# Banded-prior attention and two local layers on one core: how a head's result reaches the output projection

## What is computed

```
Q, K, V = (layernorm(x) @ W.T + b), each split into 16 heads of 16
scores  = Q K^T / 4 + lambda * gaussian_mask      (2048 x 2048 for each of 4 x 16 heads)
out     = softmax(scores) V                       (heads side by side again: 2048 x 256)
x1      = x + out @ Wo.T + bo
```

## Time and profile before

| | us |
|---|---|
| median of 3 runs | 5806.74 (5804.14 to 5806.75) |
| the profiled execution | 5799.5, span 5797.7 |
| TensorE busy in the span | 5625.3 |
| VectorE busy | 4845.0 |
| ScalarE busy | 3783.4 |
| GpSimd busy | 2148.8 |
| granted TensorE clock, mean | 0.992 |
| attention loop with its tail | to about 3188 |

### The profile page before, as it was taken

How to read it: one execution, slowest core, us unless ns; L and a number is a source line. 1 busy time by engine, 2 the same in 40 slices (tenths; PEclk the granted TensorE clock), 3 DMA queues, 4 the chain that set the end, 5 groups by cost and what they waited for, 6 DMA issues and landing times. The chain is left out here.

```text
span 5797.7 us, 159698 instructions
## 1 busy us (share of the span) xinstructions
PE 5625.3 (97%) x66524; PEld 3530.3 (61%) x66524; DVE 4845.0 (84%) x10062; ACT 3783.4 (65%) x6455; POOL 2148.8 (37%) x1750
## 2 busy tenths in 40 slices
PE   8999999999999999999999899999999999999999
PEld 3444444444444444444444788888787788888787
DVE  8888898888988888989996888888676888888676
ACT  4766776667766667767776677777333677777333
POOL 3111002111021110020001789988111789988222
PEclk9999999999999999999999999999999999999999
DMA  3111111111011101011010444555100454555111
GB/s 102 28 33 37 30 24 46 33 41 36 19 48 33 37 28 35 19 55 32 19 24 17 112 113 113 114 116 114 41 11 7 110 114 112 114 116 118 52 55 48
DMA packets 257796, 341.53 MB, mean 59 GB/s; under 512 B 41312, under 2 KB 160432, under 8 KB 257072
## 3 DMA queue, kind: packets, MB, share of 16 engines
q1 hardware_dynamic: 257072, 331.32, 23.6%
HBM read 103.90 MB, written 41.94 MB: 25 GB/s over the span
## 5 line engine op out<-in xcount | busy, mean ns | idle before, releaser
L640 ACT ACTIVATE a_pr<-a_w 128x1024 f32<-128x1024 f32 x2048 | 1989.0, 1022 | 772.3 <-PE a_w L508 672.6
L767 DVE TENSOR_REDUCE a_mx<-a_b 128x1 f32<-128x512 f32 x2658 | 1718.3, 685 | 212.9 <-PE a_b L489 210.8
L489 PE MATMUL a_b<-a_kp,a_qp 96*32 96x512 bf16 x16200 | 1460.8, 380 | 58.1 <-DVE a_mx L767 28.3
L508 PE MATMUL a_w<-a_qp,a_kp 99*32 99x512 bf16 x16384 | 1259.2, 379 | 3.5 <-ACT a_pr L640 3.0
L765 DVE CUSTOM_DVE_ANT_0 a_junk<-a_b,a_gw 128x512 bf16<-128x512 f32 x1392 | 954.4, 686 | 160.1 <-PE a_b L489 119.8
L538 PE MATMUL a_po<-a_pr,a_v 128*17 128x512 f32 x8192 | 1070.7, 592 | 0.4 <-ACT a_pr L640 0.4
L489 PEld LDWEIGHTS a_b<-a_kp,a_qp 96*32 96x32 bf16 x16200 | 482.1, 96 | 900.4 <-issue 356.6
L1591 POOL TENSOR_TENSOR l_p<-l_p,l_rc 128x512 f32<-128x512 f32 (+1 forms) x512 | 721.8, 1437 | 27.9 <-DVE l_rc L1489 27.7
L508 PEld LDWEIGHTS a_w<-a_qp,a_kp 99*32 99x32 bf16 x16384 | 464.8, 97 | 400.4 <-ACT a_pr L640 34.4
L898 POOL CAST a_pk<-a_nm 128x16 bf16<-128x16 f32 x64 | 12.6, 197 | 1774.3 <-DVE a_nm L773 1774.3
L1236 PE MATMUL l_G<-l_wqkv,l_hT 128*128 128x512 f32 x2304 | 618.6, 414 | 29.5 <-DVE l_hT L1432 23.1
(11 more groups left out here) (227 smaller groups left out, 8887.8 us busy)
## 6 DMA issues: line engine op xcount, KB each, us to landing
l_qs<-l_qT SPq DMA_DIRECT2D x512, 128.0 KB, 2.3
l_kh<-l_kT SPq DMA_DIRECT2D x512, 128.0 KB, 2.4
l_kl<-l_kT SPq DMA_DIRECT2D x256, 128.0 KB, 2.4
l_tab<-in_rotary SPq DMA_DIRECT2D x128, 128.0 KB, 2.3
a_xc<-in_x SPq DMA_DIRECT2D x28, 512.0 KB, 3.5
q_parts<-raw SPq DMA_DIRECT2D x32, 384.0 KB, 2.5
k_parts<-raw SPq DMA_DIRECT2D x32, 384.0 KB, 2.5
a_qp<-q_parts SPq DMA_DIRECT2D x64, 192.0 KB, 3.7
```

The lines of the kernel that those rows point to most:

```text
L489: m = eng.matmul(bk[32 * r:32 * r + 32, :], qp[s][0:96, o:o + 32], kp[s][0:96, c * 512:c * 512 + 512], start=True, stop=True)
L508: m = eng.matmul(wide[u][32 * r:32 * r + 32, c * 512:c * 512 + 512], kp[s][0:99, o:o + 32], qp[s][0:99, u * 1024 + c * 512:u * 1024 + c * ...
L640: eng.activation(pr[(2 * n + u) % NP][:, :], wide[u][:, :], ACT.Exp, scale=0.25).then_inc(s_exp[u], 1)
L767: t = eng.tensor_reduce(mx[g % 2][:, qb, c:c + 1], banks[i], X, ALU.max)
```

## The change

- `osb` is no longer transposed. `heads(g)` on SP sends it by five DMAs: the denominators to a row set of `sm` (one row for each head and range), and the 16 rows of sums of each range to `at[b % 2]`, whose rows are now the channels, in the form that the output projection takes as its stationary operand. `at` is double, in the last 32 tiles of `xs`. `finish_T` and `out_T` go, and with them ScalarE's `out_T` copies. ScalarE's copy of the next head waits for the five DMAs.
- `inverses(b)`, once per batch on VectorE, four steps after the last head: the reciprocal of 128 x 256 denominators, split into three bf16 parts (five instructions).
- `spread`: 24 bf16 matmuls of 256 columns with a 0/1 matrix (`pick`, made once by GpSimd) bring each head's inverse to its 16 channel rows; VectorE multiplies `at` with the bank, in place.
- `spread` and `out_project` stand on neighbouring steps, each pair eight steps after the last, from step 8. VectorE's part of `out_project` is cut in three.
- The next batch's units start at step 78 instead of 32 and are 2 to 3 steps apart instead of 4.

```diff
@@ unit_steps
-            n = n0 + 2
+            n = n0 + 8
             for w0 in range(0, W, 2):
-                n = plan(n, "out_T", b - 1, w0)
-                n = plan(n, "out_project", b - 1, w0)
+                n = plan(n, "spread", b - 1, w0) + 1
+                n = plan(n, "out_project", b - 1, w0) + 7
         if b + 1 < NB:
-            n = n0 + 32
+            n = n0 + 78
             for j in range(4):
-                n = plan(n, "stats", b + 1, j) + 3
-                for what in chunk_units(b + 1, j):
-                    n = plan(n + 3, *what) + 1
+                n = plan(n, "stats", b + 1, j) + 4
+                for k, what in enumerate(chunk_units(b + 1, j)):
+                    n = plan(n, *what) + 2 + k % 2
@@ attention_tables, the loop over steps
-        if out_at(n):
-            t.take(("out", out_at(n) - 1), ring)
@@ attention
-    at = xs[:, (NB - 1) * W:NB * W, :]
+    at = [xs[:, i * W:i * W + W, :].rearrange("p (a w) d -> p a (w d)", w=2) for i in (NB - 2, NB - 1)]
@@ tensor
+        def spread(what):
+            _, b, w0 = what
+            bk, full = claim(what)
+            pe.wait_ge(s_pick, 1)
+            pe.wait_ge(s_rp, 5 * (b + 1))
+            for c in range(2):
+                for k in range(3):
+                    for r in range(4):
+                        o = 16 * (8 * w0 + 8 * c) + 32 * r
+                        m = eng.matmul(bk[32 * r:32 * r + 32, c * 256:c * 256 + 256], picks[:, o:o + 32], rp[:, k, :], start=k == 0, stop=k == 2)
+            m.then_inc(full, 1)
         def out_project(what):
...
-            src = hT_in(what, ("out_T", b, w0))
+            i, k = slot["spread", b, w0]
+            pe.wait_ge(s_free[i], k)
+            src = at[b % 2][:, w0 // 2, :]
...
-            if out_at(n):
-                finish_T(("out", out_at(n) - 1))
@@ scalar, the copy of po
-                    i, k = slot["out", g - 1]
-                    act.wait_ge(s_full[i], k)
+                    act.wait_ge(s_heads, HEAD * g)
@@ vector
+        def inverses(b):
+            dve.wait_ge(s_heads, HEAD * HA * (b + 1))
...
+            eng.reciprocal(rsum, sm[b % 2][:, :]).then_inc(s_rp, 1)
...
+            eng.tensor_copy(rp[:, 0, :], rsum).then_inc(s_rp, 1)
...
+            eng.tensor_tensor(rless[:, :], rsum, rp[:, 0, :], ALU.subtract).then_inc(s_rp, 1)
...
+            eng.tensor_copy(rp[:, 1, :], rless[:, :]).then_inc(s_rp, 1)
...
+            eng.tensor_tensor(rp[:, 2, :], rless[:, :], rp[:, 1, :], ALU.subtract).then_inc(s_rp, 1)
+        def spread(what):
+            _, b, w0 = what
+            i, k = slot[what]
+            x = at[b % 2][:, w0 // 2, :]
             dve.wait_ge(s_full[i], k)
+            eng.tensor_tensor(x, x, banks[i], ALU.mult).then_inc(s_free[i], 1)
@@ vector, the loop
             pass1(n, 1)
-            if after:
-                out_project(after)
-                after = None
+            if out_unit(n - 1):
+                out_project(out_unit(n - 1))
+            if out_unit(n - 2):
+                out_moments(out_unit(n - 2))
             pass1(n, 2)
...
             pass1(n, 3)
-            if out_at(n):
-                finish_T(("out", out_at(n) - 1))
+            if out_unit(n - 1):
+                out_stats(out_unit(n - 1))
+            if n in units and units[n][0] == "spread":
+                spread(units[n])
+            if n % S == 5 and n > S:
+                inverses(n // S - 1)
@@ sync
+        def heads(g):
...
+            sp.wait_ge(s_osb, g + 1)
+            o, r0 = h // 8 * 256, 16 * (h % 8)
+            eng.dma_start(sm[b % 2][h:128:16, :], osb[DA:128:32, :].rearrange("p (a q) -> p a q", a=2)).then_inc(s_heads, 16)
+            for j in range(4):
+                eng.dma_start(at[b % 2][r0:r0 + DA, 2 * j:2 * j + 2, o:o + 256],
+                              osb[32 * j:32 * j + DA, :].rearrange("p (a q) -> p a q", a=2)).then_inc(s_heads, 16)
...
         for n in range(-LEAD, NS + 1):
+            if out_at(n):
+                heads(out_at(n) - 1)
             if n in packs:
                 pack(packs[n])
```

More of the change, by code:

```diff
@@ L352, in attention @@
     row = sb("row", [48, 128], BF16)
-    rc = sb("rc", [128, 4, 4])
+    sm = [sb(f"sm{i}", [128, 256]) for i in range(2)]
+    rless, rp = sb("rless", [128, 256]), sb("rp", [128, 3, 256], BF16)
+    rsum, bv_wide = junk[:, :].bitcast(F32), rless[:, :].rearrange("p (c n) -> p c n", c=2)
+    pick = sb("pick", [128, 128, 16], BF16)
+    picks = pick[:, :, :].rearrange("p a b -> p (a b)")
     bank = [ph.ps(f"b{i}", [128, 512]) for i in range(3)]
@@ L548, in rows_T @@
             m.then_inc(full, 1)
-        def finish_T(what):
-            bk, full = claim(what)
-            pe.wait_ge(s_osb, what[1] + 1)
-            for s in range(4):
-                m = eng.transpose(bk[:, s * 128:s * 128 + 128], osb[:, s * 128:s * 128 + 128], ident[:, :])
-            m.then_inc(full, 1)
         for what in first_units():
@@ L652, in scalar @@
         act.wait_ge(s_wqk, 64)
[L653 removed]
+        work = dict(turned=turned, values=values, project=project)
         for what in first_units():
@@ L742, in out_project, with out_stats, out_moments @@
             eng.tensor_tensor(x2, banks[i].rearrange("p (w d) -> p w d", d=D), x2, ALU.add).then_inc(s_free[i], 1)
+        def out_stats(what):
+            _, b, w0 = what
+            i, k = slot[what]
             dve.wait_ge(s_free[i], k)
             for w in range(2):
-                t = eng.bn_stats(st[:, w, :], x[:, i0 + w, :])
-            dve.wait_ge(s_dve, step.on(t))
+                t = eng.bn_stats(st[:, w, :], xc_of(chunk(what))[:, w0 % 4 + w, :])
+            step.on(t)
+        def out_moments(what):
+            _, b, w0 = what
+            i0 = w0 % 4
+            dve.wait_ge(s_dve, step.n)
             if 8 * b + w0 // 2 > 1:
@@ L829, in vector @@
         dve.wait_ge(s_setup, 3)
-        after = None
+        out_unit = lambda n: units[n] if n in units and units[n][0] == "out_project" else None
         for n in range(-LEAD, NS + 1):
@@ L833, in vector @@
             pass1(n, 1)
[L834 to L836 removed]
+            if out_unit(n - 1):
+                out_project(out_unit(n - 1))
+            if out_unit(n - 2):
+                out_moments(out_unit(n - 2))
             pass1(n, 2)
[L838 to L846 removed]
+            if n in units and units[n][0] == "stats":
+                stats(units[n])
+            pass1(n, 3)
+            if out_unit(n - 1):
[4 more added lines that the diff above has]
+                inverses(n // S - 1)
+        inverses(NB - 1)
+        spread(("spread", NB - 1, 0))
         for w0 in range(0, W, 2):
+            if w0 + 2 < W:
+                spread(("spread", NB - 1, w0 + 2))
             out_project(("out_project", NB - 1, w0))
+            out_stats(("out_project", NB - 1, w0))
+            out_moments(("out_project", NB - 1, w0))
             if w0:
@@ L951, in gpsimd @@
                     normal(units[n + 1])
-                if units[n + 1][0] == "out_T" and units[n + 1][2] % 4 == 0:
+                if units[n + 1][0] == "spread" and units[n + 1][2] % 4 == 0:
                     biased(units[n + 1][1], units[n + 1][2] // 4)
@@ L1082, in sync @@
                 rows_T(("rows", rows_at(n) - 1))
+        heads(NB * HA - 1)
         for w0 in range(0, W, 2):
```

84 lines of the change are left out of this document (33 added, 51 removed).

## The result

| | before | after |
|---|---|---|
| median | 5805.7 (7 runs) | 5789.98 (7 runs, 5784.48 to 5792.1) |
| ratio of the medians | | 0.9974 [0.9964, 0.9984] |
| the profiled execution's span | 5797.7 | 5783.4 |
| attention: start of the first copy of a head | 142.03 | 145.62 |
| the same, last head | 3160.37 | 3135.66 |

A forecast was written before the change was run, and what follows sets the result against it. TensorE and VectorE bound the kernel in a closed loop over PSUM banks, both nearly full. Terms -44.2 + 19.0 (pairs) + 9.0 + 5.1 + 10.0 = -1.1 us against the median 5806.7 gave 5806, range 5782 to 5823.

The forecast's parts named there:

- The transposes: Head ends: removing each head's transposes and VectorE's reciprocal and product saves 0.71 us for 62 heads; -44.2 in all.
- rival (c): Transposes' 0.71 us does not come back, since head copy or pack DMAs end the wait: +44 and up, 5850; chance 0.02.
- The spread and its stall: Spread, 24 times: matmuls 0.64 us, plus TensorE stalling 1.0 for the bank that VectorE's late product holds.
- The weight loads: Spread's matmuls: if their weight loads lie bare, 1.28 us instead of 0.64, adding 15, 5821; chance 0.03.
- The cut block: VectorE's add, statistics and moments after a projection, in three pieces: TensorE loses 0.93 us beyond the 0.34 already there.
- The walk around the ring: PSUM banks followed after a projection, reductions of 0.63: statistics cost 0.1 and 0.4, moments 0.4; 1.27 with the 0.34.
- rival (a): VectorE keeps up: spread's bank free in time and cut block absorbed; -40 in full, 5782 in half form; chance 0.31.
- rival (b): Each of the cut block's three pieces meets a full VectorE: projection 3.7 us, +17, 5823; chance 0.16.
- The inverses: Three VectorE blocks in the loop, 3.3 us each with 0.3 spared: +9.0 (4 to 10); reciprocal 1.85.
- Statistics: Next batch's statistics blocks, now three steps later after projections: TensorE stands 1.57 instead of 1.00; +5.1 us (0 to 8).
- The tail: After the last head's copy: projection starts 5.7 us later, six further products add 4.3; +10.0 (7 to 14).
- The start: GpSimd's copy for the 0/1 matrix lies in its idle time before the loop: 0.

The follow-up runs named there:

- Experiment 1: Changed kernel, but VectorE takes the spread's product before the step's last pass-1 reduction, in bank-filling order: 5771.02 us, 0.9941.
- Experiment 2: Changed kernel, but add, statistics and moments of a projection stand in one piece again: 5797.92 us, 0.9988.
- experiment 7: Changed kernel with inverses in six pieces on steps 4, 6, 8, 10, 12, 15 and output work from step 16: 5783.83 us, 0.9966.
- experiment 9: Kernel before, with only the next batch's units at their new places: 5799.72 us, 0.9993; or old spacing from step 36: 5802.24, single run.
- experiment 8: Changed kernel, but GpSimd makes `pick` ahead of its work on the first four chunks: 5785.04 us, 0.997.
- experiments 1 to 4 and 8: Changed kernel with product first (1), uncut block (2), pairs on neighbouring steps (3, 5808.61 us), neighbouring plus uncut (4, 5798.32), early `pick` (8).
- the best kernel: Changed kernel with product before the last reduction, `pick` made early, and inverses in six pieces with output work from step 16: 5762.33 us, 0.993.

## Why the prediction was right or wrong

- **The transposes** (-44.2): right. 43.79 became 43.09 in each head, SP's five DMAs and the q/k loads behind them cost nothing, and rival (c) is out.
- **The spread and its stall** (0.64 + 1.0): right, 0.65 and 0.94. Experiment 1 shows the cause, which is an order alone, and takes it away. But the sign that I gave for it was wrong: I wanted a spread step of about 4.3 us and called 3.3 a proof against me. The spread step is 3.31, and the stall falls in the step behind it, since the group that waits there belongs to that step. The weight loads do not lie bare: 24 matmuls with a load each add 0.65 to a step. The rule that I cited from the Trainium skill, TensorE: Matmul & The Clock Gate, section The mechanism, does not hold for this shape.
- **The cut block** (0.93 after the 0.34): mis-sized, 0.53. This is the step that failed first. The walk around the ring gave the statistics 0.1 and 0.4 and the moments 0.4 on top; the steps show 0.17 and 0.36 in all. It let the moments' delay come on top of the lag that the statistics had left, in full; which of TensorE's operations takes it up was not tried. Experiment 2 has the uncut block at 1.00. So cutting is worth 0.47 a pair, and a pair costs +0.33 instead of +0.79: **+8 instead of +19**. Neither rival (a), complete absorption, nor rival (b), full price, is what happened: it lies between the forecast and (a).
- **The inverses** (+9.0): 2.77 twice and 4.45 once, +10.0. The block is as forecast (3.23 us, forecast 3.3); that the clock may fall behind it was not in the sum. Its reciprocal took 1.74 us instead of 1.85: with the 0.55 us of 64 columns in experiment 7 that is 6.2 ns a column, where a reduction of 512 columns takes 0.63 us, 1.2 ns a column. That is a factor of about five. I wrote that the slope of the earlier trace rows agrees with the eight repeats that the Trainium skill states in VectorE: DVE Perf Modes, section First, the fixed hardware budget; these rows don't bear that out. (Five operations of 0.35 us also make 1.75, not the 1.9 that I gave a quick reciprocal; the sum did not use it.)
- **Statistics** (+5.1): wrong in sign. What is left of the loop's 28.3, once -44.0, +8.0 and +10.0 are taken, is -2.3, and experiment 9 finds -2.8 for the new places alone. I had taken the row at 186.28 as the price of any block standing alone, 1.57 and more; it stands where one head ends. In experiment 9 a block alone costs 1.52, and at the new places, where it stands alone too, 1.12 to 1.25: the price goes by the place. The twelve blocks together cost about 15.2 before and 14.3 after; the rest of the -2.3 lies with the other units.
- **The tail** (+10.0): 10.4, from terms that miss in opposite ways. The first add is 7.8 later instead of 5.7: SP needs 0.6 us for an issue of this kind, not 0.4, and the first spread and product add 1.0 more than I gave them. The further adds lose 3.1 instead of 4.3: five of their seven distances are 3.11, the first and the last stay at 2.5.
- **The start** (0): wrong in its reason. I costed GpSimd's copy at nothing since GpSimd was idle; VectorE paid, with a cast that took 1.58 us longer, and what of that reached the loop is not told. The Trainium skill says in SBUF — State Buffer, section Who interferes with whom, that VectorE and GpSimd share a port pair which one instruction holds to its end, and that a cast of VectorE can be one that needs it. The rows agree: 1.81 and 1.30 us for casts of 0.23 and 0.29, each ending just behind GpSimd's instruction. Most of the 3.6 us, and perhaps all of it, is the quick start of the one profiled execution of before (experiment 8).

Against the sum of -1.1 the two profiled executions differ by -14.3: the pairs make -11, the statistics -7, the inverses +1, the start +3.6, the tail +0.4, and 0.2 are rounding.

That the time lies inside the range is in part luck. The lower end, 5782, was set for a spread whose bank is free in time, and that did not happen. Two other terms, the cut block and the next batch's units, missed in the same direction by 11 and 7 us, and the range was wide enough for both.

## What to carry to other kernels

When engines hand banks round in a ring, let the reader take them in the order in which they were filled: one operation out of order cost 0.83 us each time, more than its own length. When work is moved by a few steps in a loop with a period, look at every in-order queue that it touches, GpSimd's too, for what must leave that queue by a fixed step of the period: a shift by two steps cost 71 us here, and the "distance" gained mostly by missing that place. And price a block of work by a row from the same place in the loop: the place moved the cost of one block from 1.1 to 1.5 us.

## What the runs showed of the hardware

- A cast on VectorE that started while GpSimd worked ended only behind GpSimd's instruction: 1.81 us beside a 1.99 us cast, 1.30 beside a 2.39 us addition, against 0.23 and 0.29 alone. Not each cast does: four of 0.28 each, from 3199.53 on in the changed kernel, show no delay beside a GpSimd operation that the trace has from 3199.36 to 3202.27.
- TensorE's granted clock fell from 2.4 to 1.2 GHz behind a stall of 2.2 us in one batch of the changed kernel and not in the two others. Over the six profiles with the inverses in one piece (the changed kernel, experiments 1 to 4 and 8) it fell behind 13 of 18. In experiment 1's profile it fell after all three, and there the step of the inverses and the next cost up to 5.8 us together. This is one of its windows, whose clock is a mean of the two levels:

```profile
1650.00:1656.00 6.00, 4.69 (x46) 1.79 (x50) 5.02 (x11) 2.05 (x2) 0.00 (x0) 0.59 0.00 0
```

  What decides stays open. With the inverses in pieces at the places of experiment 7 it fell behind one of six, none in the best kernel's profile. Fewer falls are most of what the cut gains there: the inverses of the three batches, falls included, cost 15.9 us in experiment 1's profile and 6.2 in the best kernel's, of which the cutting itself makes 2. Experiment 8's profiled execution took 5792.70 us and has all three falls, that of the changed kernel took 5785.16 and has one; that the spread of the times comes from such falls is likely, but not shown.
- VectorE's reciprocal takes 6.2 ns per column and some 0.15 us: 0.55 us for 64 columns and 1.74 for 256, a little less than the slope of the 155 and 248 ns of the earlier trace rows gives (1.84).
